# A two-layer graph network on one core: the source table in four chunks, and twelve selected columns in layer 1

## What is computed

```python
# layer 0
ew = (efeat @ W_e + b_e).reshape(E, in_f, out_f)
msg = jnp.einsum('ei,eio->eo', feat[src], ew)
summed = jax.ops.segment_sum(msg, dst, num_segments=N)
neigh = summed / jnp.maximum(cnt, 1.0)[:, None]          # + bias
# layer 1
A = edge_emb[edge_type].reshape(-1, MSG_DIM, HID_DIM)
msg = jnp.einsum('emh,eh->em', A, features[edge_src])
m = jax.ops.segment_sum(msg, edge_dst, num_segments=n_nodes)
# r, z, n gates of m and features; h_new = (1 - z) * n + z * features
x = _layernorm(x + layer0(x)); x = _layernorm(x + layer1(x))
```

## Time and profile before

| what | value |
|---|---|
| median of 3 runs | 5798.82 us (5797.19 to 5807.0) |
| profiled execution | 5833.2 us, its span 5831.4 us |
| TensorE matmul, weight load | 5227.1 us (90%), 4693.1 us (80%) |
| VectorE | 4199.3 us (72%) |
| ScalarE | 3891.8 us (67%) |
| GpSimd | 3412.9 us (59%) |
| TensorE, chain that ended last | 63% |
| layer 0, layer 1 | about 37 to 2871 us, 2956 to 5759 us |

### The profile page before, as it was taken

How to read it: one execution, slowest core, us unless ns; L and a number is a source line. 1 busy time by engine, 2 the same in 40 slices (tenths; PEclk the granted TensorE clock), 3 DMA queues, 4 the chain that set the end, 5 groups by cost and what they waited for, 6 DMA issues and landing times.

```text
span 5831.4 us, 131035 instructions
## 1 busy us (share of the span) xinstructions
PE 5227.1 (90%) x41758; PEld 4693.1 (80%) x41759; DVE 4199.3 (72%) x5387; ACT 3891.8 (67%) x5533; POOL 3412.9 (59%) x3559
## 2 busy tenths in 40 slices
PE   6999999999999999999978888888888888888887
PEld 5888888888888888888767878788877788788887
DVE  7878787778777788777856666666666666666666
ACT  6666676676666666666566666666666666666664
POOL 6555565555555555555555656655655655655554
PEclk9999999999999999999989999999999999998998
DMA  3111111111111111111111111111111111111110
GB/s 66 33 30 31 33 31 31 31 31 33 30 31 33 30 31 33 31 32 31 25 23 23 23 24 23 23 23 22 23 23 23 23 23 22 24 22 23 23 23 14
DMA packets 330970, 161.25 MB, mean 28 GB/s; under 512 B 193244, under 2 KB 330011, under 8 KB 330771
## 3 DMA queue, kind: packets, MB, share of 16 engines
q1 hardware_dynamic: 218224, 130.59, 9.3%
q0 software_dynamic: 112512, 29.03, 6.3%
q10 hardware_dynamic: 160, 0.80, 0.1%
HBM read 157.44 MB, written 2.66 MB: 27 GB/s over the span
## 4 chain that ended last, share of the span: by engine, by line
PE 63%; issue 15%; DVE 12%; another core or an unknown queue 6%; DVEq 4%; ACT 0%; DMA 0%; POOL 0%; SPq 0%; ACTq 0%
PE psN L752 46%; PE psM L789 15%; DVE cand L953 6%; DVEq L997 2%; DVE nodeT L935 2%; DVE z L991 2%; DVE z L959 1%; DVEq L934 1%; DVEq L952 0%; PE psN L893 0%; PE psM L764 0%; DVEq L958 0%; PE psM L773 0%; DVE grp_hot L943 0%
## 5 line engine op out<-in xcount | busy, mean ns | idle before, releaser
L752 PE MATMUL psN<-table_hi,pick 128*128 128x320 f32 (+1 forms) x13670 | 4080.1, 316 | 167.8 <-DVE cand L953 85.3
L752 PE MATMUL psN<-table_lo,pick 128*128 128x320 f32 (+1 forms) x13670 | 3987.4, 308 | 13.7 <-issue 13.7
L752 PEld LDWEIGHTS psN<-table_hi,pick 128*128 128x128 f32 x13670 | 2598.8, 190 | 306.4 <-issue 226.1
L578 ACT ACTIVATE pick<-dist 128x640 fp32r<-128x640 bf16 (+1 forms) x2485 | 1790.5, 784 | 1336.8 <-PE psN L752 852.8
L752 PEld LDWEIGHTS psN<-table_lo,pick 128*128 128x128 f32 x13670 | 2599.6, 190 | 21.6 <-issue 21.5
L500 POOL DMA_INDIRECT z<-in_x,idx x1761 | 1704.4, 968 | 1176.9 <-issue 417.4
L500 POOL DMA_INDIRECT z<-h_rows,idx x1755 | 1682.2, 959 | 1168.3 <-issue 403.7
L570 ACT ACTIVATE dist<-src_mod,neg_node 128x640 bf16<-128x640 uint16 (+1 forms) x2485 | 1972.6, 874 | 3.3 <-DMA src_mod<-src_mod_rows 3.3
L953 DVE TENSOR_TENSOR cand<-psN,grp_hot 128x640 f32<-128x640 f32 (+1 forms) x1492 | 1122.1, 765 | 1061.3 <-PE psN L752 482.7
L991 DVE TENSOR_TENSOR z<-psD,z 128x2048 f32<-128x2048 f32 (+1 forms) x750 | 1367.8, 1824 | 55.6 <-issue 31.5
L789 PE MATMUL psM<-z,onehot 128*32 128x273 f32 (+1 forms) x12500 | 904.4, 345 | 371.4 <-issue 327.0
(11 more groups left out here) (108 smaller groups left out, 734.3 us busy)
## 6 DMA issues: line engine op xcount, KB each, us to landing
src_mod<-src_mod_rows SPq DMA_DIRECT2D x249, 192.0 KB
src_mod<-src_mod_rows SPq DMA_DIRECT2D x248, 160.0 KB
z<-in_x,idx POOLq DMA_INDIRECT x1761
z<-h_rows,idx POOLq DMA_INDIRECT x1755
eab<-in_edge_attr SPq DMA_DIRECT2D x125, 200.0 KB
idx<-in_src SPq DMA_DIRECT2D x250, 12.5 KB
dstb<-in_dst SPq DMA_DIRECT2D x250, 14.0 KB
grp<-src_grp SPq DMA_DIRECT2D x249, 5.5 KB
```

The costliest lines, as they stand in the source:

```text
L578: act.activation(pick[j][:, CHUNKS[i], 0:hi - lo], dist[i][:, 0:hi - lo], ACT.Relu, bias=1.0, scale=-1.0).then_inc(l["pick_act"], 1)
L752: mm = pe.matmul(rows[:, :, 0:cells.shape[2]], pick[j][:, c, at:at + P], cells, start=(i == 0 and part == 0), stop=(i == TC - 1 and part = ...
```

## The change

The 98 places of a partition are cut into four chunks, of 26, 26, 26 and 20 groups, in the order 0, 3, 1, 2. A column takes 8 matmuls, 6 of 416 moving columns and 2 of 320. Layer 1 selects twelve columns (19 is added) and gathers thirteen; layer 0 still selects eleven, column 19 in place of 20. The boundary between the halves moves from 5 to 6 in both layers (HCUT, HALF_1). The last pair of layer 1 is (10, 12) instead of the single column 10; layer 1's waits of the gathers are set anew.

```diff
-PICKED = [4, 5, 6, 7, 13, 14, 21, 22, 23, 24, 20]
-H = ((11, 11), (11, 11))
+PICKED = [4, 5, 6, 7, 13, 14, 21, 22, 23, 24, 19, 20]
+H = ((11, 11), (12, 12))
-HCUT = [[(0, 5, h) for h in hs] for hs in H]
+HCUT = [[(0, 6, h) for h in hs] for hs in H]
-HALF_1 = 5
+HALF_1 = 6
-FIRST_PAIRS = [(5, 6), (6, 8), (8, 10)] + ([(10, 11)] if H[1][0] == 11 else [])
+FIRST_PAIRS = [(6, 8), (8, 10), (10, 12)]
-SUMMED = [(0, 4), (4, 6), (6, 10), (10, 11)]
+SUMMED = [(0, 4), (4, 6), (6, 10), (10, 12)]
-AFTER_OWN = ([{5: 0, 6: 1, 7: 2, 8: 3, 12: 5, 13: 6}] * 2, [{6: 0, 7: 1, 10: 3, 11: 4, 13: 5}] * 2)
+AFTER_OWN = ([{5: 0, 6: 1, 7: 2, 8: 3, 12: 5, 13: 6}] * 2, [{6: 0, 7: 1, 9: 3, 10: 4, 12: 5}] * 2)
-AFTER_LAST = ([{0: 7, 1: 8, 2: 9, 4: 10}] * 2, [{0: 7, 1: 8, 2: 9, 4: 10}] * 2)
+AFTER_LAST = ([{0: 7, 1: 8, 2: 9, 4: 10}] * 2, [{0: 7, 1: 8, 2: 9, 3: 10, 5: 11}] * 2)
-TC, NG = 5, 20
-CHUNKS = (0, 1, 4, 2, 3)
+TC, NG = 4, 26
+CHUNKS = (0, 3, 1, 2)
-NG_MUL, NG_SHIFT = 205, 12
+NG_MUL, NG_SHIFT = 158, 12
-                        picks(*((3, 4) if k == 0 else (2, 3, 4)))
+                        picks(*range(3 if k == 0 else 2, TC))
-                    g0, g1 = next(g for g in SUMMED if g[0] <= t0 < g[1])
+                    g0, g1 = next((g[0], min(g[1], H[k][buf])) for g in SUMMED if g[0] <= t0 < g[1])
```

## The result

The changed kernel takes 5862.93 us (median of 4 runs, 5860.54 to 5866.92), the kernel before 5802.91 us (4 runs, 5797.19 to 5809.98): a ratio of 1.0092, 95% interval 1.0073 to 1.0111. It is slower, as forecast, but by 60 us and not by some 330, and 7 us under the low end of the range. The profiled execution is 5866.92 us with a span of 5865.0, 33.6 above the span of before.

What follows compares the result with a forecast made beforehand. TensorE's own work was taken to bound layer 0, a loop through VectorE with late signals layer 1. Layer 0's +258 and layer 1's +75 us on the profiled 5833.2 gave 6166, less 34: 6130 us; range 5870 to 6350.

Steps and rivals of the forecast that it cites:

- I take late in half of the blocks: Layer 1: the signal of column t=5 reaches VectorE late in half of the blocks, +0.6 us per block.
- What bounds the kernel: Layer 0 (22.9 us a block) is TensorE's own work; layer 1's loop (22.5) runs through VectorE, which sees t=5 late.
- Part 1: TensorE's columns, both layers: two fewer matmul starts at 13.3 ns each, 1.44 to 1.413 us, -0.3 us per block.
- The rival in which nothing is saved on the starts: 416-wide matmuls cost their columns and the same total overhead: +0.3 us per block, 6205 us; chance 0.10.
- Part 3: VectorE's products over 26 groups: +2.25 us to 20.4 per block in layer 0, +2.36 us on layer 1's chain.
- Part 5: Layer 0: transposes wait for a sums copy behind two ScalarE picks, TensorE idle 1.95 us; +1.06 us per block.
- Part 6: Layer 0: TensorE's new pause brings low-clock stretches in 6 blocks in 10, 1.0 us per block.
- The sum of layer 0: Layer 0: 1.06 us for the wait plus 1.0 for the clock per block, times 125: +258 us.
- Part 7: Layer 1: results wait for two picks and a copy; -0.43 to +2.7 us per block, +0.6 taken.
- the punctual branch: Layer 1: if t=5 is signalled on time, the block is 0.43 us shorter despite twelve columns.
- Signals punctual, clock untouched: Rival: no late signals or clock loss, +132 us in layer 0, -54 in layer 1: 5877 us; chance 0.20.
- layer 1 at TensorE's floor: Rival, not slower: layer 1 at 21.5 us a block (-125 us), layer 0 loses only 1.06: 5806 us; chance 0.08.

Runs made afterwards that it cites:

- e5: The kernel before with 3 gathers per block instead of 14, the columns left out keeping old values: 4952.42 us.
- e2: The kernel before with only the boundary between the halves moved from 5 to 6: 6174.93 us, ratio 1.0636.
- e4: The changed kernel with two small extra matmuls ahead of each column: 6753.84 us.
- e11: The changed kernel with 3 gathers per block, old values in the columns left out: 5702.21 us.
- e1: The kernel before with only the four chunks; eleven columns and boundary 5 stay: 5760.69 us, ratio 0.9922.
- e3: The changed kernel with layer 0's boundary back at 5: 5732.85 us, ratio 0.9866.
- e9: The kernel before with 3 gathers per block and three GpSimd iotas in place of each gather left out, all waits kept: 4950.83 us.
- e6: The changed kernel with layer 0's boundary at 5 and AFTER_SUMS (8, 6) instead of (9, 8): 6091.62 us, ratio 1.0496.
- e12: The changed kernel with layer 0's boundary at 5 and three of layer 0's gather waits on own columns removed: 5903.84 us, ratio 1.0174.

## Why the prediction was right or wrong, point by point

The forecast was 333 us on top of the profiled execution; the blocks make 35. Of the 298 us between them 130 lie in layer 0, where the sum block was carried over unchanged and fell by 1.39 us, and 168 in layer 1, where "I take late in half of the blocks" was wrong and the sum block fell too.

**What bounds the kernel: half right.** Layer 0 was called TensorE's own work, "the sum block is the rest of the 22.9". It was TensorE's time, but 1.84 us of that rest aren't there without the gathers (5.18 against 3.34), and in layer 1 2.60 of 4.25. The late signals of layer 1 were tied to the last gather of a run, and e5, with few gathers, has none of these waits; that the sum block belongs to the same cause was in reach, in the two pauses without a releaser of the earlier trace rows.

**Part 1, wider matmuls: wrong sign.** A column costs 1.46 us (1431.38 to 1432.84), not 1.413. After the start of a matmul of 320 the next starts 147 ns later, 13.7 over its columns, as read; one of 416 takes on average (1.460 - 2 x 0.147) / 6 = 0.194 us, 21 over its 173. The step that failed carried the price of a start at 320 over to 416. Worth +0.52 us per block of eleven columns against the forecast, 65 us in layer 0 alone. The rival in which nothing is saved on the starts was right in this. (The Trainium skill, TensorE: Matmul & The Clock Gate, section "Wait — 56ns, not 53.3ns?", has a start at about 2.5 ns above the columns. These matmuls, each with a weight load of its own, show 13.7 and 21, so the measurement decides for them; at 2.5 the column would have stayed within 0.02 us of its 1.307.)

**Part 3, VectorE: right.** Forecast 20.4 us per block of layer 0 and 18 of layer 1; the windows give 2433.65 us in 2850, 20.38 a block, and 2047.80 in 2520, 17.77. It bounds nothing, save 0.47 us per block of waiting for the last product in layer 1.

**Part 5, the wait ahead of the transposes: right.** Forecast 1.95 us, measured 1.93 to 1.94 in the changed kernel, e2, e4 and e11, gone in e1 and e3.

**Part 6, the clock: right.** Forecast 6 blocks in 10 and 1.0 us; 58 low stretches of 3.4 us in 118 blocks, 0.8 us a block. The earlier trace rows carried this one. (The Trainium skill, same page, section "HAM oscillation — how this bites in real kernels", describes a kernel that waits about 3 to 5 us for a transfer in each tile and falls to the low clock in each. The pause here is 1.94 us, shorter than any of those; the trace has a low stretch in every second block, and in e11, where the rest of the block is denser, in 91 of 118.) The two blocks in the windows above, 23.6 us at 1.00 and 24.6 at 0.93, show the price.

**The sum of layer 0: too high by 1.04 us a block.** Forecast +2.06, measured +1.02. The pause came as forecast and the clock 0.2 cheaper, the columns cost 0.5 more. The step that failed is a term that was not written: the sum block was carried over unchanged. It fell by 1.39 us, 174 us in all. The pause on TensorE shifts the columns on whose ends the gathers wait, so that after the second gather in the rows above GpSimd stands still for 3.01 us and the sum block has one gather near it. e2 has the same pause and the same fall (4.20); e1 and e3 have neither (5.34, 5.32). That moving layer 0's boundary does it is shown (e3 against the changed kernel); that it does so through the pause and the place of the gathers is argued, not shown: it is the reading that fits e4, e5, e9 and these rows, though e6 and e12 say that the number near the block is not the whole of it.

**Part 7, layer 1: the punctual branch came, not the mixture.** Forecast for a punctual t=5: the results wait 0.35 us, and a block of 21.9 us at full clock; measured 0.38 and 21.87. The wait was understood; that the block fits so well is luck. The forecast had 14.9 us from t=5 to the next sum block and 3.95 for the sum block, the traces have a mean of 16.46 and 2.38: columns of 1.460, 0.47 us of waiting for VectorE and slower results on one side, a sum block 1.6 us shorter on the other. TensorE and ScalarE in such a block:

```profile
4113.01 1.69 PE L789 MATMUL psM<-z,onehot 128*32 128x128 f32 x46 [0.39 <-DVE z L991]
...
4122.00 0.49 PE L773 MATMUL psM<-sumT,A 128*128 128x128 f32 x2 [0.39 <-ACT sumT L557]
```

```profile
4120.22 1.58 ACT L578 ACTIVATE pick<-dist 128x768 fp32r<-128x768 bf16 x2 [4.41 <-PE psN L752]
4121.70 0.24 ACT L557 COPY sumT<-psM 128x128 f32<-128x128 f32 x1
```

ScalarE takes up the picks just after t=5 (t=6 starts at 4120.02) and the results wait for two picks and a copy, as worked out. The step that failed is "I take late in half of the blocks": the signal is late in none of 118, and where +0.6 was forecast, -0.74 is measured, 168 us over the layer (some of it, as said, the low clock in the profiled execution of before). The forecast priced the late signal rightly, as e2 shows (2.03 us), but guessed how often it comes. Of the gain the sum block is the largest part: four chunks alone bring it from 4.25 to 2.94, and the rest of the change to 2.38 (the boundary alone: 4.44). With the pauses went 25 of 26 low stretches, which had cost 0.6 us a block. Why four chunks alone shorten it is not settled; e1 has one gather near where before has two, which fits, but I can't say what moved it.

**The rivals.** "Signals punctual, clock untouched", 5877 us, lies 14 us from the result, and for a wrong reason: the clock was not untouched. Punctual signals in layer 1 were right. The rival on the other side, layer 1 at TensorE's floor, gave 5806 with a block of 21.5; layer 1 came within 0.4 us of it. For layer 0 it has +1.06 without a clock loss, and +1.02 is measured with one, paid for by the shorter sum block: luck again. The other differences are layer 1's 0.26 us a block and the 30 us of the profiled execution. e3, which leaves layer 0's boundary alone, gets its gain in layer 1 (21.90) without a loss in layer 0.

**The range** was too narrow below. It allowed for costs that don't come, but no term in it was a gain from a shorter sum block, although two pauses in the earlier trace rows were there to be lost.

## What to carry to other kernels

Before a stretch of small matmuls is counted as work, subtract its pauses without a releaser and ask what else runs beside them: here a shift of TensorE by two microseconds went with 1.4 us less in that stretch, and one gather more near it with 1.4 us more. Where a wait was worked out on the path (the copy behind two picks), the number held; what is not on that path, how transfers and bursts fall against each other, came only from runs, and belongs into the range on both sides. A boundary that one stage needs should be moved in that stage alone: the same edit in layer 0 cost 130 of the 5863 us.

## What the runs showed of the hardware

- Gathers that GpSimd issues (L500) slow TensorE, without sharing an engine or a wait with it: 50 small matmuls take 3.34 us (273 columns) or 1.65 us (128 columns) with no gather near, and up to 6.88 and 4.44 with them, in part in pauses that have no releaser (0.85 of the 1.84 us that layer 0 of before has above 3.34), in part in gaps under 0.15 us. Eleven gathers per block cost 850 us of 5800, in this, in late signals and in low stretches. Iotas in their place cost nothing (e9).
- The large matmuls (L752) are hardly slowed by them: from one of 320 columns to the next the median is 147 ns with 14 gathers (before) and with 3 (e5), and pauses without a releaser between them are 0.1 us per block before.
- What it is in a gather that stops TensorE, its descriptors, its packets or the signals at its end, no run here tells, nor why the sum block is longest behind an unbroken row of gathers (e12). The pauses keep no fixed distance from a gather's start either: of those over 0.15 us in layer 0, 129 of 163 end 1.5 to 1.95 us after one in before, 21 of 351 in e12.
- A matmul of 416 columns costs 21 ns above its columns on average and one of 320 14 ns, start to start at full clock.
- A pause of TensorE of 1.94 us in each block brings a stretch of 3.4 us at half the clock in 58 of 118 blocks, in 91 of 118 in e11, and in 2 of 118 where it is absent (e3).
